# Feed-forward on one core: where the statistics and the copy of the sums of x stand in the iteration

## What is computed

```python
x = x + 0.5 * _L0_ffn_ref(_layernorm(x), gate, up, down)   # feed-forward, first run
x = x + _L0_attn_ref(_layernorm(x), ...)
x = x + 0.5 * _L0_ffn_ref(_layernorm(x), gate, up, down)   # the same weights, second run
x = x + 0.5 * _L1_ffn_ref(_layernorm(x), ...)              # mixture of experts
x = x + _L1_attn_ref(_layernorm(x), ...)
x = x + 0.5 * _L1_ffn_ref(_layernorm(x), ...)
```

```python
def fp4_linear(x, w):              # both rounded in blocks of 16 to 0, .5, 1, 1.5, 2, 3, 4, 6 times a scale
    return einsum('bsk,nk->bsn', fp4_quant_dequant(x), fp4_quant_dequant(w))
gate, y = fp4_linear(x, w_gate), fp4_linear(x, w_up)       # 128 -> 352
return fp4_linear(silu(gate) * y, w_down)                  # 352 -> 128
```

## Time and profile before

| what | value |
|---|---|
| median of 3 runs | 1439.05 us |
| lowest, highest | 1435.94, 1440.18 us |
| the profiled execution's own time | 1442.13 us |
| its span, first to last instruction | 1440.4 us |
| busy share PE, DVE, ACT, POOL | 78%, 64%, 57%, 44% |
| mean granted TensorE clock | 0.90 of full |
| first feed-forward, `largest` of z = 0 to the last statistics | 39.9 to 180.3 us |
| second feed-forward, the same | 444.3 to 579.1 us |

### The profile page before, as it was taken

The page is one execution under the profiler, slowest core; times in us unless marked ns, Lnnn a source line. Parts: engine busy times, 40 slices in busy tenths (PEclk is TensorE's granted clock), DMA queues, the critical chain, the costliest instruction groups (busy, mean ns, idle before and its releaser), DMA issues.

```text
span 1440.4 us, 33720 instructions
## 1 busy us (share of the span) xinstructions
PE 1117.6 (78%) x11264; PEld 863.8 (60%) x11265; DVE 915.1 (64%) x1715; ACT 825.8 (57%) x1442; POOL 638.3 (44%) x922
## 2 busy tenths in 40 slices
PE   0577749999995777379999915899998836999991
PEld 0355526666663555269999902455555426999991
DVE  5799648888856887743333365888999475333333
ACT  0455326677764453266666652667776625666665
POOL 3422244434401222036766613676677402767660
PEclk9999858999997998769999955999999966999995
DMA  8100013332210000101111132343223010111115
GB/s 251 40 1 0 1 44 62 55 61 52 67 26 0 1 0 1 58 21 49 47 47 46 49 122 59 61 68 79 64 59 75 17 59 19 49 48 47 47 47 182
DMA packets 160689, 74.96 MB, mean 52 GB/s; under 512 B 125451, under 2 KB 152852, under 8 KB 160596
## 3 DMA queue, kind: packets, MB, share of 16 engines
q1 hardware_dynamic: 151508, 55.06, 16.3%
q0 software_dynamic: 9088, 18.63, 4.4%
HBM read 28.03 MB, written 15.73 MB: 30 GB/s over the span
## 4 chain that ended last, share of the span: by engine, by line
PE 56%; DVE 21%; issue 7%; ACT 5%; DMA 5%; SPq 3%; POOL 3%; DVEq 1%; ACTq 0%; POOLq 0%
PE PS L1011 18%; PE PS L1039 9%; PE PS L668 4%; DVE m L794 4%; PE PS L385 3%; PE PS L376 3%; PE PS L634 3%; SPq L896 3%; PE PS L596 3%; PE PS L650 2%; DMA qT<-qs 2%; DVE sg L794 2%; ACT pt L1114 1%; PE PS L676 1%; PE PS L622 1%
## 5 line engine op out<-in xcount | busy, mean ns | idle before, releaser
L1011 PE MATMUL PS<-xTs,pt 128*128 128x128 f32 x2272 | 281.2, 278 | 0.0
L1011 PEld LDWEIGHTS PS<-xTs,pt 128*128 128x128 f32 x2272 | 269.8, 195 | 0.0
L742 ACT ACTIVATE pt<-PS 128x768 f32<-128x768 f32 (+1 forms) x256 | 225.7, 915 | 49.7 <-PE PS L596 24.4
L1156 DVE TENSOR_TENSOR pt<-pt,PS 128x512 f32<-128x512 f32 x142 | 97.6, 687 | 234.3 <-PE PS L1011 180.9
L1284 POOL DMA_INDIRECT xs<-rows,src x142 | 137.6, 969 | 153.5 <-DVE src L1150 110.9
L1073 ACT ACTIVATE pt<-wgu 128x1024 f32 x142 | 149.9, 1057 | 88.2 <-issue 81.2
L1294 POOL DMA_INDIRECT outs<-ys,dst x142 | 139.9, 985 | 94.6 <-DVE ys L1171 87.5
L794 DVE TENSOR_REDUCE m<-PS 128x4 f32<-128x1024 f32 x128 | 153.1, 1220 | 28.5 <-PE PS L596 25.7
L1039 PE MATMUL PS<-wdn,pt 128*128 x1136 | 150.2, 275 | 1.2 <-DVE ys L1171 1.2
L794 DVE TENSOR_REDUCE sg<-PS 128x6 f32<-128x768 f32 x128 | 118.1, 954 | 35.1 <-PE PS L596 33.0
L1039 PEld LDWEIGHTS PS<-wdn,pt 128*128 128x128 f32 x1136 | 138.0, 192 | 1.5 <-issue 1.5
(11 more groups left out here) (241 smaller groups left out, 2156.3 us busy)
## 6 DMA issues: line engine op xcount, KB each, us to landing
pt<-outs SPq DMA_DIRECT2D x16, 512.0 KB, 4.9
rows<-qT SPq DMA_DIRECT2D x12, 256.0 KB, 2.2
xs<-rows,src POOLq DMA_INDIRECT x142, 2.5
outs<-ys,dst POOLq DMA_INDIRECT x142, 2.3
wgu<-in_L_ffn_w_gate SPq DMA_DIRECT2D x1, 2048.0 KB
wgu<-in_L_ffn_w_up SPq DMA_DIRECT2D x1, 2048.0 KB
wdn<-in_L_ffn_w_down SPq DMA_DIRECT2D x8, 256.0 KB
out<-X SPq DMA_DIRECT2D x8, 256.0 KB, 4.6
```

Source lines behind the costliest of these rows:

```text
L742: s.activation(k.pt[:, a % 4, :, 0:w], k.PS[:, self.bank:self.bank + 2, 0:w], ACT.Exp, scale=self.scale).then_inc(self.s_p, 1)
L1011: last = t.matmul(k.PS[:, 1 + 2 * p + w, c * P:(c + 1) * P], k.wst[:, 1 - p, w, c * P:(c + 1) * P], k.xTs[:, p, :], start=True, stop=True)
L1156: v.tensor_tensor(k.hs[:, p, :], k.sgs[:, p, :], k.PS[:, 2 + 2 * p, :], ALU.mult).then_inc(self.s_h, 1)
```

## The change

On VectorE the statistics move from between `largest` and `scaled` to between `scaled` and the product, and from pair z - 5 to pair z - 6. On ScalarE the copy of the new x moves from the end of iteration z, for pair z - 3, to the middle of the next one: behind the squares, in front of the two copies for down, for pair z - 4. The walk has one iteration more (`STEPS` is N + 6), in which VectorE takes the statistics of the last pair. No instruction is added, removed or resized.

```diff
-    STEPS, FIRST = N + 5, 6
+    STEPS, FIRST = N + 6, 6
@@ Ffn.vector, fn(z, p)
             if self.group(z):
                 largest(z, p)
-            if self.has(z - 5):
-                eng.wait_ge(self.s_added, x0 + z - 4)
-                for j in range(2):
-                    bn_stats(k, 2 * (z - 5) + j)
             if self.group(z):
                 scaled(z, p)
+            if self.has(z - 6):
+                eng.wait_ge(self.s_added, x0 + z - 5)
+                for j in range(2):
+                    bn_stats(k, 2 * (z - 6) + j)
             if self.has(z - 2):
                 eng.wait_ge(self.s_up_ps, x0 + z - 1)
@@ Ffn.scalar, fn(z, p)
             squared(z + 1, 1 - p)
+            if self.has(z - 4):
+                eng.wait_ge(self.s_y_ps, x0 + z - 3)
+                s.activation(k.X[:, ds(2 * (z - 4), 2), :], k.PS[:, 7, 0:256].rearrange("p (a b) -> p a b", a=2),
+                             ACT.Copy).then_inc(self.s_added, 1)
             if self.has(z - 3):
                 eng.wait_ge(self.s_hqT_ps, x0 + z - 2)
...
-            if self.has(z - 3):
-                eng.wait_ge(self.s_y_ps, x0 + z - 2)
-                s.activation(k.X[:, ds(2 * (z - 3), 2), :], k.PS[:, 7, 0:256].rearrange("p (a b) -> p a b", a=2),
-                             ACT.Copy).then_inc(self.s_added, 1)
```

## The result

Five runs of the changed kernel gave a median of 1429.26 us (1426.21 to 1431.45), five of the kernel before 1439.05 (1435.24 to 1440.18): ratio 0.9932, 95% interval 0.9915 to 0.9950. A second comparison, with eight and eighteen runs, gave 1429.59 against 1436.93 us: 0.9953 (0.9933 to 0.9973). So the medians differ by 7 to 10 us.

The account below looks back on a forecast made before the run. The prediction took GpSimd's multiplications, with L288 ending just behind them, to bound the feed-forward loop. Terms of -1.84 us (first feed-forward) and -1.98 (second) gave -3.8, from 1439.05 to 1435.2 us; range 1430.8 to 1441.0.

Parts of the forecast that it names:

- What bounds the kernel, and the front: In the feed-forward loop L288 can't end before GpSimd, ending 0.05 us behind it; moving statistics out of the front wins nothing.
- Statistics next to the product: On VectorE between L290 and L312, z = 6 to 17, the moved statistics cost +0.94 us per feed-forward.
- z = 5 of the second feed-forward: There L288 ended at 472.77, GpSimd at 471.58; without the wait the iteration was to gain -1.14 us.
- The end up to down 14: In z = 16 to 18, L288 goes back to GpSimd's end, less the costs of moved statistics and copy.
- -0.93 in z = 17: L288 in z = 17 goes back to 0.05 us behind GpSimd's end: -0.93 us in both feed-forwards.
- The copy's price, 0.29: ScalarE's moved copy delays the copies for down: covered in the loop, +0.29 us once at each feed-forward's end.
- -2.14 and -1.14 for z = 18: L288 in z = 18 goes back to GpSimd's end: -2.14 us in the first feed-forward, -1.14 in the second.
- The step that failed: From down 14 through down 15 to the last statistics, the old chain shifts as a whole, with no further gain.
- rival B: TensorE's clock stays up for one to three of downs 14 and 15: -5.2 to -8.0 us in all; chance 0.23.
- C: VectorE's instructions don't overlap around the product: total +2.4 us, 1441.4; chance 0.11.
- D: TensorE loses its clock inside the loop: +2.7 us per iteration, three such bring the total to +4.3, 1443.4; chance 0.07.
- E: L288 doesn't wait for GpSimd: 0.30 us in some twenty iterations, -6 more, 1429; chance 0.03.

## Why the prediction was wrong

**What bounds the kernel, and the front: right.** In the first feed-forward L288 ends 0.04 to 0.05 behind GpSimd in z = 4 to 16 of the kernel before and in z = 4 to 18 of the changed one, with or without statistics ahead of it; its semaphores ask only for GpSimd's work of iteration z - 2. (In z = 8 of the second feed-forward it ended 0.25 behind in the kernel before, which I hadn't read; that gain pays for the loop there.) The Trainium skill (SBUF — State Buffer, "Who interferes with whom") names such a reason: a VectorE `tensor_scalar` can take the port pair that it shares with GpSimd, and whichever comes second waits for the other's whole instruction. The trace agrees in that L288 takes 0.68 to 1.26 us in these iterations of the changed kernel, instead of the 0.17 behind GpSimd's end, and ends with GpSimd; no run here took the multiplications away from GpSimd.

**Statistics next to the product: right, a little too dear.** +0.03 in even iterations where I had 0.08, nothing in odd ones, and in z = 16 and 17:

```profile
153.29 0.89 DVE L290 SCALAR_TENSOR_TENSOR q_xn<-xh,q_inv 128x704 f32<-128x704 f32 x1
154.10 0.48 DVE L188 BATCH_NORM_STATS2 bn<-X 128x6 f32<-128x128 f32 x2
154.50 0.87 DVE L306 TENSOR_TENSOR qT<-sg,PS 128x704 f32<-128x704 f32 x1
155.28 0.88 DVE L312 SCALAR_TENSOR_TENSOR q_xn<-q_mg,q_xn 128x704 f32<-128x704 f32 x1
```

155.28 - 153.29 = 1.99 (2.01 forecast). From the product's start to the next start it is 0.78, so the product, which reads PSUM, holds VectorE as briefly as I took it (0.80). The 0.86 that I worked out from the Trainium skill (VectorE: DVE Perf Modes, "The TRN2 errata") is an estimate; the row's own duration, 0.87, agrees with it, but the next instruction starts before that is over. In place of 0.94 per feed-forward the first paid about 0.65: 0.11 over z = 6 to 13, 0.06 in z = 14 and 15, 0.25 and 0.24 in z = 16 and 17.

**z = 5 of the second feed-forward: right for the profile that I read.** -1.14 forecast; the iteration fell from 8.40 to 7.27. In the other two profiles of the kernel before it took 7.48 and 8.66, so the term is 0.2 to 1.4, by the execution.

**The end up to down 14: right in its sum for the profile that I read.** -0.93 in z = 17 came as forecast (6.50 to 5.81, with 0.24 paid in it). From the start of z = 16 to down 14 I had 0.52 - 0.93 - 2.14 + 0.29 = -2.26 in the first and 0.52 - 0.93 - 1.14 + 0.29 = -1.26 in the second; the two profiles give 17.07 - 19.39 = -2.32 and 17.07 - 18.40 = -1.33. The copy's price, 0.29, is measured at 0.27 to 0.28. But the -2.14 and -1.14 for z = 18 come in large part from down 13 at the low level, not from the order as such: with the clock held in both orders down 14 comes only 17.77 - 17.07 = 0.70 and 17.87 - 17.07 = 0.80 earlier.

**The step that failed:** "behind it the chain down 14, transposes, L430, L431, down 15, copy, last statistics is the old one and shifts as a whole". It doesn't: from the start of down 14 to the next phase it is 8.14 us instead of 11.61 in the first feed-forward and 7.25 instead of 9.10 in the second, -3.47 and -1.85 in this pair of profiles. By the means of three profiles each it is 10.53 - 8.14 = 2.39 and 8.82 - 7.25 = 1.57, 4.0 us that the sum puts at nothing. I took the durations of TensorE's instructions as given, though the change shortened the very idle time ahead of them, and with TensorE kept busy in that time their clock stayed at 1.00. The rival B had this mechanism and its price, -5.2 to -8.0 in all; the feed-forwards brought 7.65. That its total fits is in part luck: it took 3.8 for the waits and 1.4 to 4.2 for the clock, and the runs show about 2.7 and 5.0. What was wrong is its chance, 0.23. The point against it was one row, a down 15 at the low level behind 0.95 us of idle time; but that down stands behind a down 14 which was itself low behind 3.38 us. In the eleven other ends of before and after down 15 is high behind the same 0.95.

**The range.** Its low end, 1430.8, took in B at the three downs that were low in the profile. The first comparison lies 1.5 us below it, the second, in proportion (1439.05 x 0.9953 = 1432.3), inside. What the first shows beyond the feed-forwards' 7.65 us isn't in the feed-forwards; the attention scatters between 255.49 and 259.67 in the profiles without regard to the change, and so hides or adds a microsecond or two.

**The other rivals.** C (no overlap around the product) is excluded by 2.26; D (the clock falls in the loop) by loops of 58.94 and 59.16 us against 58.83 and 59.25, at a granted clock of 1.00 (84.65 to 136.30 us); E by L288 itself, though its figure, 1429, is by accident the median of the first comparison.

## What to carry to other kernels

When a change shortens the time that TensorE waits, work out its instructions behind that wait at both clock levels: here the wait itself was worth 1 us per feed-forward and the clock that came with it about 2.5. Idle time charged to a wait in the groups by line (29.7 us here) says little before it is compared with an iteration that lacks the waiting instruction. And when a change has three parts, try them singly: here either of two, the place of the statistics or their lag, was enough, and the third, the copy, gave nothing. Read more than one profile, too, before a wait is taken as a fixed price: the one in z = 18 of the first feed-forward was 2.14 us in the profile that I read and 1.2 and 1.0 in the two others.

## What the runs showed of the hardware that was not expected

TensorE's clock made an earlier start a later end: with the lag alone down 14 of the first feed-forward started 0.75 us sooner than in the changed kernel, fell to the low level behind 2.13 us of idle time, and the feed-forward ended 0.36 us later (25.58 against 25.22). With matmuls of no use in the idle time the same order ended at 24.75. Across the ends an idle time of 2.12 to 3.38 us ahead of down 14 always went with the low level, while ahead of down 13 2.40 us went with either.

The slow level of one TensorE stretch also set the price of a wait on another engine: L288 in z = 18 ended 2.19 us behind GpSimd when down 13 ran low, and 0.57 when it ran high, kept there by matmuls of no use.
